# Moving four of sixteen score tiles' copies and splits from VectorE to ScalarE, and V's and X's steps to other slots, in a four-stage cross-attention and feed-forward kernel

## What is computed

```python
attn = einsum('bhqd,bhkd->bhqk', qh * scale, kh) + add_attn   # L0, heads of 64
attn = softmax(where(mask == 0, NEG_INF, attn)); out = attn @ vh
x = ln(out @ w_o + residual)
...
x = _ln(x + _mha(x, x, sa_..., mask), ln1_g, ln1_b)           # SA, heads of 32
x = _ln(x + _mha(x, memory, ca_..., None), ln2_g, ln2_b)      # CA, heads of 32
h = relu(_linear(x, ff_w1, ff_b1))
x = _ln(x + _linear(h, ff_w2, ff_b2), ln3_g, ln3_b)
```

## Time and profile before

| | us |
|---|---|
| median of 3 runs | 4072.25 |
| the profiled execution | 4070.64 |
| its span in the profile | 4068.8 |
| busy in the span: TensorE, VectorE, ScalarE, GpSimd | 3861.5, 3055.5, 2264.5, 1865.6 |
| mean granted TensorE clock | 0.987 |

### The profile page before, as it was taken

The page is one execution under the profiler, slowest core; times in us unless marked ns, Lnnn a source line. Parts: engine busy times, 40 slices in busy tenths (PEclk is TensorE's granted clock), DMA queues, the critical chain, the costliest instruction groups (busy, mean ns, idle before and its releaser), DMA issues.

```text
span 4068.8 us, 64484 instructions
## 1 busy us (share of the span) xinstructions
PE 3861.5 (95%) x21468; PEld 3013.1 (74%) x21468; DVE 3055.5 (75%) x6362; ACT 2264.5 (56%) x5059; POOL 1865.6 (46%) x1905
## 2 busy tenths in 40 slices
PE   9999999999999989999999998888899979999999
PEld 7888888888888866666666765666666658888887
DVE  7777777788888889999999878888888863333334
ACT  7666667666666656666666665566666541111111
POOL 5343344333433346667767665666766641001101
PEclk9999999999999999999999999999999989999999
DMA  4334333121112246666666456666756572011100
GB/s 140 136 124 134 121 124 119 64 65 63 55 55 78 73 129 162 174 166 171 167 171 169 126 150 158 169 179 177 179 144 154 148 217 97 32 37 50 39 31 32
DMA packets 587543, 486.09 MB, mean 119 GB/s; under 512 B 405968, under 2 KB 405968, under 8 KB 586192
## 3 DMA queue, kind: packets, MB, share of 16 engines
q1 hardware_dynamic: 569424, 431.63, 38.2%
q10 hardware_dynamic: 17792, 50.33, 3.5%
HBM read 197.68 MB, written 188.22 MB: 95 GB/s over the span
## 4 chain that ended last, share of the span: by engine, by line
PE 35%; POOL 9%; DVE 7%; issue 5%; ACT 3%; DMA 3%; SPq 1%; POOLq 0%; DVEq 0%; ACTq 0%
POOL QS L2321 7%; PE psV L1478 4%; PE psS L1410 3%; PE psS L1357 3%; PE psS L1355 3%; PE psS L1356 3%; PE psT L1432 3%; PE psJ L1355 2%; PE psJ L1357 2%; PE psJ L1356 2%; PE psT L1355 2%; PE psT L1357 2%; PE psT L1356 2%; ACT PR L1764 2%; DMA RAW<-x 2%
## 5 line engine op out<-in xcount | busy, mean ns | idle before, releaser
L2321 POOL TENSOR_SCALAR QS<-QK 32x1024 fp32r<-32x1024 f32 (+2 forms) x1152 | 1244.2, 1080 | 897.9 <-DVE QK L1970 420.4
L1764 ACT ACTIVATE PR<-PR,MN 128x512 f32<-128x512 f32 x1536 | 1102.9, 718 | 524.4 <-DVE MN L1951 265.1
L1951 DVE CUSTOM_DVE_ANT_0 PR<-psS,RAW 128x512 f32<-128x512 f32 x1024 | 694.7, 681 | 258.5 <-PE psS L1407 192.4
L1432 PE MATMUL psT<-ID,PR 128*128 128x128 f32 x4680 | 714.3, 275 | 36.9 <-ACT PR L1764 29.3
L1432 PEld LDWEIGHTS psT<-ID,PR 128*128 128x128 f32 x4680 | 569.4, 142 | 180.6 <-ACT PR L1764 64.3
L1410 PE MATMUL psS<-QS 128*128 128x512 f32 x1024 | 475.8, 465 | 75.7 <-DVE PR L1955 31.9
L1776 ACT ACTIVATE R<-psT 128x512 fp32r<-128x512 f32 x512 | 304.5, 595 | 324.2 <-PE psT L1432 322.8
L1955 DVE TENSOR_SCALAR_CACHE_REDUCE PR<-psS 128x512 f32<-128x512 f32 x512 | 346.5, 680 | 77.4 <-PE psS L1410 75.5
L1796 ACT ACTIVATE PR<-psS,COLS 128x512 f32<-128x512 f32 x128 | 88.3, 690 | 546.6 <-PE psS L1357 541.6
L1410 PEld LDWEIGHTS psS<-QS 128*128 128x128 f32 x1024 | 196.6, 192 | 259.7 <-issue 131.4
L2034 DVE CAST QK<-PR 128x512 fp32r<-128x512 f32 x128 | 57.7, 450 | 395.1 <-ACT PR L1796 349.6
(11 more groups left out here) (148 smaller groups left out, 9085.5 us busy)
## 6 DMA issues: line engine op xcount, KB each, us to landing
split_rows<-RAW SPq DMA_DIRECT2D x192, 256.0 KB, 2.6
split_rows<-plain SPq DMA_DIRECT2D x174, 256.0 KB, 2.5
x<-Y SPq DMA_DIRECT2D x96, 256.0 KB, 2.3
RAW<-x SPq DMA_DIRECT2D x96, 256.0 KB, 3.8
W<-kept ACTq DMA_DIRECT2D x12, 2048.0 KB, 11.3
Y<-x SPq DMA_DIRECT2D x96, 256.0 KB, 3.6
kept_c<-R SPq DMA_DIRECT2D x32, 512.0 KB, 5.0
kept<-ROWS SPq DMA_DIRECT2D x32, 512.0 KB, 3.1
```

Of the source, the lines that this page charges most:

```text
L1432: mm = nc.tensor.transpose(dst[:, kt * P:(kt + 1) * P], prob(st, k)[:, kt * P:(kt + 1) * P], ID[:, :])
L1764: nc.scalar.activation(prob(st, k), prob(st, k), ACT.Exp, bias=MN[:, k % 8:k % 8 + 1], scale=-1.0, accum_out=row_sums(st, SM, g)[:, qt, j: ...
L1951: nc.vector.tensor_tensor_reduce(out=prob(st, k), in0=psS[:, n % 2], in1=FB[:, k % NT], scale=-st.scale, scalar=BIG, op0=ALU.add, op1=ALU. ...
L2321: nc.gpsimd.tensor_scalar(to, pair, 1.0, 1.0, ALU.mult, ALU.mult).then_inc(stacked, 1)
```

## The change

ScalarE makes the splits of tiles 2 and 8 of each sixteen, and counts them on a semaphore of their own (`p_split_act`), on which `BOUNCE` and the `MAX` of three tiles on wait. ScalarE copies five of the ten turned tiles, 3, 7, 11, 12 and 14, VectorE the other five. V's second half moves to slots 18.5 to 22 and 44.5 to 47.5, X's turns from 51, 51.75, 52.5, 53.25 to 49, 50, 51, 53, and the load of x's last tile from slot 51.6 to 49.4. `C_TAKE` stays at 51.5.

```diff
 SENT = (0, 2, 4, 6, 8, 10)
+SPLIT_BY_ACT = (2, 8)
+COPIED_BY_ACT = (3, 7, 11, 12, 14)
...
-        ("V", 1, 0): ((44.5, 45, 46, 47), 47.5, 47.5),
-        ("V", 1, 1): ((47.75, 48, 49, 50), 50.5, 50.5),
+        ("V", 1, 0): ((18.5, 19.5, 20.5, 21.5), 22, 22),
+        ("V", 1, 1): ((44.5, 45.5, 46.5, 47), 47.5, 47.5),
...
-    "X_TURN": (-13, -12.25, -11.5, -10.75),
-    "X_HI": (-12.75, -12, -11.25, -10.5),
-    "X_LO": (-12.5, -11.75, -11, -10.25),
-    "LOAD_X": (-30, -28, -26, -12.4),
+    "X_TURN": (-15, -14, -13, -11),
+    "X_HI": (-14.75, -13.75, -12.75, -10.75),
+    "X_LO": (-14.5, -13.5, -12.5, -10.5),
+    "LOAD_X": (-30, -28, -26, -14.6),
...
-            return grouped(st) and k % 8 in (0, 3, 6)
+            return grouped(st) and k % 16 in COPIED_BY_ACT
...
+        split_at, splits = {}, {p_split: 0, p_split_act: 0}
+        for tile in orders["SPLIT"]:
+            by = p_split_act if tile[2] % 16 in SPLIT_BY_ACT else p_split
+            splits[by] += 1
+            split_at[tile] = by, splits[by]
...
-                sp.wait_ge(p_split, n + 1)
+                sp.wait_ge(*split_at[tile])
...
+            def split_prob(st, k, b):
+                tile = st.name, b, k
+                n = sent_at[tile]
+                act.wait_ge(exp_done, exp_at[tile])
+                if n >= 4:
+                    act.wait_ge(bounced[n % 4], times(n - 4))
+                nc.scalar.activation(halves(tile).rearrange("p (h k) -> p h k", h=2),
+                                     prob(st, k).bitcast(U16).rearrange("p (k h) -> p h k", h=2),
+                                     ACT.Copy).then_inc(p_split_act, 1)
...
-                    dve.wait_ge(p_split, sent_at[before] + 1)
+                    dve.wait_ge(*split_at[before])
...
-                    elif step == "SPLIT":
+                    elif step == "SPLIT" and k % 16 not in SPLIT_BY_ACT:
```

More of the change, by code:

```diff
@@ L703 @@
     ('first', 3): {
-        ('LOAD_X', 0, 'CA', 1): 30, ('LOAD_X', 1, 'CA', 1): 30.5, ('LOAD_X', 2, 'CA', 1): 39.1, ('LOAD_X', 3, 'CA', 1): 51.7,
+        ('LOAD_X', 0, 'CA', 1): 30, ('LOAD_X', 1, 'CA', 1): 30.5, ('LOAD_X', 2, 'CA', 1): 39.1, ('LOAD_X', 3, 'CA', 1): 49.5,
         ('JOB', (('OUT', 2), 0), 'SA', -1): 18, ('JOB', (('OUT', 2), 1), 'SA', -1): 18.5, ('JOB', (('OUT', 2), 2), 'SA', -1): 19,
@@ L881, in build @@
         p_split = sem("p_split")
+        p_split_act = sem("p_split_act")
         bounced = [sem(f"bounced{i}") for i in range(4)]
@@ L1804, in run @@
                             tal["s"].mark("pairs")
+                    elif step == "SPLIT" and k % 16 in SPLIT_BY_ACT:
+                        split_prob(st, k, batch + off if at is None else at)
                     elif step == "P_HI":
```

## The result

The changed kernel takes **4015.07 us** (median of 4 runs, 4013.61 to 4017.45) against 4072.1 us for the kernel before: a ratio of 0.9857, with a 95% interval of 0.9844 to 0.9869, or 57 us less. The forecast was 4048, 24 us less. The direction and the range (3995 to 4083) held, the size did not: it was less than half of what came. One of the six executions of a kernel further down, e2, ran at a granted clock of 0.81 and took 4465 us; it is left out of e2's median.

What follows compares the result with a forecast made beforehand. TensorE bounds the kernel, with small holes in SA and CA and CA's wait for x's load; -48.8 - 5.5 + 30 (2.0 us in 15 batches) = -24.3 from 4070.6 gives 4046.3, as median 4048 us, range 3995 to 4083.

Steps and rivals of the forecast that it cites:

- (1): CA's slots 52 to 55: x's last load leaves ahead of the 2 MB `C_TAKE`, TensorE's wait goes, 48.8 us gained.
- (2): CA's longest `MAX` waits, slot 42 behind tile 40's split: 1.1 us less in five batches, 5.5 us gained.
- (4): ScalarE's queue: copy and split delay the exponentials of tiles 9, 25, 41, 57, costing 5.4 us a batch, other splits 0.6.
- (6): V's and X's new slots: slots 48 to 51 lose 1.1 us a batch, V's job in slots 18 to 21 0.
- (3): Engine time per batch: VectorE from 100.2 to 87.5 us, ScalarE from 73.7 to 86.7, a ScalarE split 1.04 us.
- (5): VectorE's queue relieved: `MAX` waits 3.4, hole ahead of `PV` 0.65, other holes 1.0, together 5.1 us gained a batch.
- other holes: TensorE's remaining small holes in a batch, 2 us, of which half, 1.0 us, was to go through VectorE's relief.
- The two small terms of (5): V's job in slots 18.5 to 21.5 filling the hole ahead of `PV`, 0.65 us, and half the other holes, 1.0.
- ScalarE becomes the late engine: Rival, chance 0.17: ScalarE's delays are not paid back, +4.5 us a batch, 4085 us.
- VectorE's relief in full: Rival, chance 0.2: the exponentials' delay hides behind existing holes, a batch gains 2 us, 3988 us.
- The load still late: Rival, chance 0.07: x's load still lands late, behind bulk data or the buffer's wait, 49 us stay, 4097 us.

Runs made afterwards that it cites:

- e2: Kernel before with only the move of two splits and the copies to ScalarE, slots of V, X and the x load as before: 4055.3 us.
- e4: Changed kernel with the load of CA's kept weight tile (`KEEP_LOAD`) two slots earlier, at 49.5, in CA's batches 1 to 4: 4001.6 us.
- e8: e4 with ScalarE's splits of tiles 8, 24, 40 and 56 cut to an eighth of their columns: 3968.9 us.
- e7: e4 with no work moved to ScalarE: all splits on VectorE, ScalarE's old copies: 4037.7 us.
- e1: Kernel before with only the new slots of V, X and the x load, splits and copies as they were: 4041.5 us.
- e14: e4 with ScalarE's old copies and the splits of tiles 2, 6 and 8 on ScalarE: 3961.7 us.
- e5: e4 with ScalarE's old copies, the splits of tiles 2 and 8 still on ScalarE: 3990.6 us.
- e15: e5 with the split of tile 48 on ScalarE too: 3993.2 us.
- e11: e4 with ScalarE splitting tiles 2 and 4 instead of 2 and 8, and making its old copies plus tile 12's: 4015.0 us.
- e12: e4 with ScalarE's old copies and only the split of tile 8 of each sixteen on ScalarE: 3992.5 us.
- e13: e4 with ScalarE's old copies and only the split of tile 2 of each sixteen on ScalarE: 4031.5 us.

## Why the prediction was right and wrong

**(1) The x load: right in mechanism, 14.7 us too large.** The load left 2.1 us ahead of the 2 MB (I had said 3 to 4), TensorE's wait is gone, and batches 5 and 6 are at 8.9 us. What failed is "nothing else of SyncE's queue is put in front of it ... and those behind it wait for nothing that the load delays": I looked at what stands ahead of and behind the x load and not at what the shift of `C_TAKE` itself does to `KEEP_LOAD`, 0.6 us ahead of it before. e4 shows both: with that load earlier 13.5 us come back (1.6 of them by the clock of batch 0), and the stretch then gains 48.3. `C_TAKE` itself takes 9.4 to 11.3 us where I had 9.2, and no engine waits for it.

**(2) CA's longer `MAX` waits: in the right direction.** They fell from 27.2 us to 4.9 in CA's batches 0 to 6. What part is the 5.5 us I put down was not measured apart. Outside slots 52 to 55 these seven batches gained 14.7 us, where (2) and the 2.0 us a batch of (4) to (6) together had them lose 8.5.

**(3) Engine time: right within 2 us a batch.** ScalarE's split takes 1.05 us (I had 1.04), by this row of the changed kernel's groups:

```profile
L1783 ACT ACTIVATE plain<-PR 128x1024 uint16<-128x1024 uint16 x58 | 60.9, 1050 | 0.3
```

A batch has 89.5 us of VectorE and 84.7 of ScalarE, forecast 87.5 and 86.7.

**(4) ScalarE's queue: the delay right, its price too high.** Around tile 9 of SA's batch 4 the timeline shows the chain as forecast: copy of tile 7, split of tile 8, exponential, and TensorE 1.00 us late.

```profile
1935.56 0.58 ACT L1794 ACTIVATE plain<-psT 128x512 f32<-128x512 f32 x1
1936.04 1.05 ACT L1783 ACTIVATE plain<-PR 128x1024 uint16<-128x1024 uint16 x1
1936.98 0.71 ACT L1774 ACTIVATE PR<-PR,MN 128x512 f32<-128x512 f32 x1
...
1937.84 0.66 PE L1442 MATMUL psT<-ID,PR 128*128 128x128 f32 x4 [1.00 <-ACT PR L1774]
```

The waits for exponentials went from 1.2 to 5.8 us a batch, close to the 6 forecast. But by e8 a microsecond of it costs 0.7: about 4 us and not 6. (The sum itself had a slip: 4 x 1.43 less 4 x 0.1 is 5.3 and not 5.4.)

**(5) VectorE's relief: with (4) the step that failed.** I let 3.4 us of waits for `MAX` go, the ones that show as idle time of the matmuls. TensorE also waits with a weight load in hand, and then the matmul ahead reads as busy or the wait reads as "issue". These are the rows of TensorE on `psS` in that batch that name `MAX` or nothing, before:

```profile
PEld psS L1410 <- issue: 8.7, 11, 1.5
...
PEld psS L1410 <- DVE MN L1951: 4.8, 8, 0.8
...
PE psS L1410 <- DVE MN L1951: 3.4, 5, 1.1
```

and after (there is no third row of a size):

```profile
PEld psS L1420 <- DVE MN L1973: 4.4, 6, 0.8
...
PEld psS L1420 <- issue: 1.2, 2, 0.8
```

Weight loads overlap with matmuls, so these sums are not lost time one for one. But measured from the starts in the two traces, against the shortest step between each pair of matmuls, the score was late by 6.8 us in this batch before and by 1.1 to 1.3 after: some 5.5 us of relief where I had 3.4. With (4) at 4 us the move gains 1.5 us a batch, and e2 and SA's steady batches of e4 against e7 (109.2 against 110.7) have 1.3 to 1.5. The two terms are read in two ways, though, one from starts and one from e8, so only their sum is measured. Forecast for the move in (4) and (5): 6.0 - 3.4 - 1.0 = +1.6. A difference of 2.9 us in 15 batches is 43 us. That is more than the whole error of some 30 us on the span; step 1's 14.7 us the other way hid a third of it. (4) was 2.0 too high and the `MAX` waits of (5) 2.1 too low; the 1.0 of other holes, which no trace shows, takes a part of that back.

The two small terms of (5) had no ground that shows. The waits of `PV` for VectorE's copy are 10.6 us in six batches of the changed kernel where they were 10.7, so V's job did not fill that hole. And the "other holes, 2 us" hold the 1.2 us of waits for exponentials, which (4) makes longer; 0.8 were left to gain from, and I took 1.0.

**(6) The slots: the sum about right, by luck in part.** +1.1 in (6) less 0.65 in (5) is +0.45; e1 has +0.3 to +0.4. Slots 48 to 51 take 6.95 us in e1, close to the 5.7 + 1.1 of the forecast. But V's job, for which I had put 0, makes slots 20 to 27 of e1 14.7 us long where they were 13.7, and slots 52 to 55 give 0.55 us back.

**The rivals.** *ScalarE becomes the late engine* did not happen, though its cause did: the exponentials are late as it says. The Trainium skill's rule (page "ScalarE: Activation LUTs", section "Rules for kernel authors") that simple element-wise work belongs on VectorE would have kept these splits there, which is 36 us worse here (e7 against e4) and 76 worse than e14 by the medians, 31 and 73 by the ratios. The rule prices the instruction, and rightly (1.05 us against 0.83 in the mean of the changed kernel's VectorE splits); what the queue in front of it is worth it does not say. *VectorE's relief in full* came closest: 2 us a batch gained where 1.1 were, and its reason, holes that are there anyway, holds for the third of the delay that e8 found free. That GpSimd quickens too, as it has it, was not measured apart. *The load still late* returned in another load's clothes.

## What to carry to other kernels

When work moves from one queue to another, price the place that it frees by what is queued behind it there, and count the waits of weight loads with those of matmuls. Of a delay on a queue that is not the only late one, two thirds were paid here and not all. When a step is moved past a bulk transfer, look at every small transfer that was just ahead of that bulk transfer, not only at the one that the move is for.

## What the runs showed of the hardware

**A small load just behind a bulk transfer waits for all of it.** By the landings in the traces, the 256 KB of a load issued 1.3 us or more ahead of the 2 MB took 2.5 to 4.2 us; issued 0.6 us ahead 2.6 to 3.1 in seven cases and 10.7 in one; issued 0.27 us ahead 2.5 and 3.0 in two cases and 9.8 to 11.1 in seven; and issued behind it 7.6 to 11, about as long as the 2 MB itself (8.1 to 11.3). The Trainium skill (page "DMA: Bandwidth & Descriptors", section "Queues, rings and completion order") has each DMA engine take turns between its queues, a packet at a time; by that the small load would land early. Here it lands with the end of the bulk one, and the measurement decides.

**VectorE and GpSimd hold each other up, and a tie goes one way or the other.** Two batches of e5, both with VectorE's split of tile 48 and a GpSimd instruction begun within 20 ns of each other:

```profile
1784.49 1.59 POOL L2343 TENSOR_SCALAR QS<-QK 32x1024 fp32r<-32x1024 f32 x1 [0.44 <-PE psS L1420]
1784.50 0.69 DVE L2096 COPY plain<-PR 128x1024 uint16<-128x1024 uint16 x1
...
1892.73 2.49 POOL L2343 TENSOR_SCALAR QS<-QK 32x1024 fp32r<-32x1024 f32 x2 [0.43 <-PE psS L1420]
1892.75 1.58 DVE L2096 COPY plain<-PR 128x1024 uint16<-128x1024 uint16 x1
```

In the first GpSimd's instruction stretches from 1.04 to 1.59 us and the split keeps its 0.69; in the second the split takes 1.58. The Trainium skill's page "SBUF — State Buffer" (section "SBUF: two separate sides") has it that, of a VectorE instruction in a two-port mode and a GpSimd instruction, the one that starts first keeps the other out for its whole length. The trace agrees that one of the two is stretched; both records show GpSimd's instruction starting first, by 10 and by 20 ns, and yet it is the stretched one in the first batch, so the trace does not say who came first.

The price of the tie is read where the clock is full: e5's batches with the short split take 108.3 us, two with the long one 109.1. The 110.8 us of the third is the tie's 0.8 and 1.7 more that came with a lower clock. With tile 48's split on ScalarE (e15) five of six SA batches are within 0.4 us of each other, but at 108.7 to 109.0, and their slots 48 to 51 take 7.1 us, as with the long split (7.2) and not as with the short one (6.3). So the run removed the tie, kept its cost, and by its own second expectation did not remove the long batch: one of 110.9 us is still there.

**The clock can fall or stay behind the same hole.** In e15, SA's batches 1 and 2 run alike on TensorE to some 10 ns for 27 us up to the `PV` behind slot 50, with the same 1.44 us of idle time ahead of it. Then the windows read:

```profile
1676.30:1680.00 3.70, 3.51 (x17) 0.75 (x18) 2.55 (x7) 2.46 (x5) 1.34 (x2) 0.56 0.53 188
1786.80:1789.00 2.20, 2.01 (x17) 0.57 (x18) 2.20 (x7) 1.87 (x5) 1.35 (x2) 1.00 0.18 63
```

The same 17 matmuls take 3.5 us at a granted clock of 0.56 and 2.0 at 1.00, and the batches take 110.9 and 108.7 us. The clock also fell in the batch of 110.8 us of e5 (0.93 and 0.89 in slots 48 to 55) and in three of e7 (0.80 to 0.83 in slots 48 to 51, where the others have 1.00).

The fall goes with the split of tile 48. Take batches 1 to 6 of SA and of CA in the traces of all kernels but e15, 192 batches. Where VectorE's split of tile 48 is short (0.68 to 0.75 us, 146 batches), the clock of slots 48 to 51 is 1.00 every time. Where it is long (1.52 to 1.58 us, 46 batches), it is below 1.00 in 13. What tips it in these, with the same work and the same hole ahead, stays open. I take it for why kernels here differ by some microseconds from run to run, and why e1, e7, e11, e12 (3987 to 4003 us) and e13 are known less well than the intervals say.
